# Attention 0 of a two-layer adaLN block: each group of values issued in two halves, copies of V and of the output turns moved by a slot or two

## The reference, cut to what matters

```python
h = _layernorm(x) * (1 + ca) + sa
q = (h @ Wq + bq).reshape(B, S, H, Dh)
latent = h @ Wl + bl
k = (latent @ Wk + bk).reshape(B, S, H, Dh)
v = (latent @ Wv + bv).reshape(B, S, H, Dh)
scores = einsum('bihd,bjhd->bhij', q, k) * SCALE
attn = softmax(scores)
out = einsum('bhij,bjhd->bihd', attn, v).reshape(B, S, D) @ Wo + bo
x = x + ga * out
```

## Time and profile before

| what | us |
|---|---|
| median of 3 runs | 915.63 |
| lowest and highest run | 914.82, 916.39 |
| the profiled execution | 914.76 |
| its span, first to last instruction | 912.9 |
| busy in the span: PE, DVE, ACT, POOL | 751.2, 623.3, 574.9, 326.9 |

### The profile page before, as it was taken

How to read it: one execution, slowest core, us unless ns; L and a number is a source line. 1 busy time by engine, 2 the same in 40 slices (tenths; PEclk the granted TensorE clock), 3 DMA queues, 4 the chain that set the end, 5 groups by cost and what they waited for, 6 DMA issues and landing times. The chain is left out here.

```text
span 912.9 us, 17945 instructions
## 1 busy us (share of the span) xinstructions
PE 751.2 (82%) x6002; PEld 546.6 (60%) x6002; DVE 623.3 (68%) x1509; ACT 574.9 (63%) x1285; POOL 326.9 (36%) x412
## 2 busy tenths in 40 slices
PE   3466888888588874679999999589999985999996
PEld 3222444444244333579999998467777764887874
DVE  3075787787577826677777775357676855888885
ACT  0214777777477774548888887377767743555553
POOL 3541324224221000140000000367778552776674
PEclk9999999999899997779999999789999986999999
DMA  5354353443865020000000000000000070355430
GB/s 135 34 59 49 54 55 44 53 52 48 157 121 61 8 34 17 1 1 1 1 1 1 1 1 2 1 1 2 2 1 1 3 188 4 104 146 154 114 107 23
DMA packets 78221, 42.05 MB, mean 46 GB/s; under 512 B 8649, under 2 KB 76082, under 8 KB 78002
## 3 DMA queue, kind: packets, MB, share of 16 engines
q1 hardware_dynamic: 78130, 40.89, 24.4%
HBM read 25.66 MB, written 2.24 MB: 31 GB/s over the span
## 5 line engine op out<-in xcount | busy, mean ns | idle before, releaser
L563 DVE TENSOR_REDUCE att_negmax<-att_p_max 128x2 f32<-128x512 f32 x256 | 164.6, 685 | 85.0 <-PE att_p_max L443 84.1
L647 ACT ACTIVATE att_probs<-att_p_sT 128x1024 f32<-128x1024 f32 x128 | 129.3, 1021 | 56.0 <-PE att_p_sT L449 55.1
L443 PE MATMUL att_p_max<-att0p_QK 48*128 48x256 bf16 x512 | 91.9, 290 | 36.8 <-DVE att_negmax L563 12.0
L2141 POOL TENSOR_TENSOR moe_z_lo<-moe_z,moe_z_hi 128x512 fp32r<-128x512 f32 x64 | 96.7, 1523 | 54.9 <-ACT moe_z_hi L2094 54.1
L449 PE MATMUL att_p_sT<-att0p_QK 51*128 51x256 bf16 x512 | 85.6, 279 | 1.2 <-DMA att0p_QK<-att_maxT 1.2
L933 PE MATMUL ffn0s_p_h<-ffn0s_u_hi,ffn_h_hi 128*128 128x256 f32 x256 | 71.5, 313 | 18.1 <-DVE ffn0s_u_lo L1200 12.8
L443 PEld LDWEIGHTS att_p_max<-att0p_QK 48*128 48x128 bf16 x512 | 33.6, 97 | 86.8 <-DVE att_negmax L563 47.4
L472 PE MATMUL att_p_o<-att_probs,att0p_V 128*32 128x256 f32 x1024 | 70.2, 393 | 9.5 <-ACT att_probs L647 8.4
L1200 DVE TENSOR_TENSOR ffn0s_g_lo<-top_raw,ffn0s_g_hi 128x512 fp32r<-128x512 f32 x64 | 50.4, 804 | 38.4 <-ACT ffn0s_g_hi L1145 37.1
L2132 DVE TENSOR_TENSOR moe_z<-moe_act_u,top_raw 128x512 f32<-128x512 f32 x64 | 73.7, 1151 | 2.2
L729 POOL TENSOR_TENSOR att_rstd<-att_var_eps,top_minus_half 128x2 f32<-128x2 f32 x16 | 11.5, 719 | 172.3 <-DVE att_var_eps L556 172.3
(11 more groups left out here) (273 smaller groups left out, 2047.6 us busy)
## 6 DMA issues: line engine op xcount, KB each, us to landing
top_raw<-combine SPq DMA_DIRECT2D x32, 512.0 KB, 6.5
att0p_QK<-att_parts SPq DMA_DIRECT2D x192, 64.0 KB
top_X<-in_L_attn_x SPq DMA_DIRECT2D x4, 512.0 KB, 6.9
top_raw<-in_L_ffn_h_w SPq DMA_DIRECT2D x2, 1024.0 KB
out_x<-top_X SPq DMA_DIRECT2D x8, 256.0 KB, 2.3
top_wo_all<-gates SPq DMA_DIRECT2D x1, 1024.0 KB, 5.9
prep_wmod<-in_L_wmod SPq DMA_DIRECT2D x2, 384.0 KB, 3.6
top_raw<-in_L_ffn_w_w SPq DMA_DIRECT2D x3, 256.0 KB
```

The costliest lines, as they stand in the source:

```text
L443: mm = pe.matmul(p_max[u % 2][:, i, :], QK[r][rows, g, 0, i * P:(i + 1) * P], QK[r][rows, g, 1, :], start=True, stop=True)
L563: dve.tensor_reduce(negmax[:, :, w, g], p_max[u % 2][:], AX.X, ALU.max, negate=True).then_inc(maxed, 1)
L647: act.activation(probs[g % 2][:, t % 2], p_sT[t % 2][:], ACT.Exp).then_inc(exped, 1)
L2141: pool.tensor_tensor(z_lo[e % RING][:], z[e % RING][:], z_hi[e % RING][:].bitcast(F32), ALU.subtract).then_inc(z_lo_ready, 1)
```

## The change

Three tables get new entries, and `pe_pv` gets an argument j, the key tile, so that one call issues four of the eight matmuls of a group. The waits of the group stand ahead of its first half, the signal behind its second.

- PE, values: group 0 of batch s from slot 11 to slots 11 and 12; group 1 from slot 15 to slot 15 and slot 0 of the next step; group 2 from slot 3 to slots 3 and 4; group 3 from slot 7 to slots 7 and 8. The score tiles of the later slot stand between the halves.
- PE, turns: turn of O1 from slot 9 to 10, turn back from 11 to 12, out from 12 to 13, turn of y from 14 to 15.
- DVE: second normalisation of O from ahead of tile 10 to ahead of tile 11.
- ACT: copy of V from slot 7 to 9, which is from ahead of exp1 to behind it; OTn from 11 to 12, y from 12 to 13. OT0 from slot 11 to 12, behind exp3; OT1 from slot 15 to slot 0 of the next step, behind exp5; OT2 from slot 3 to 4, behind exp7; OT3 from slot 6 to 8, behind exp1.

```diff
-PES = {"ln": 0, "max_turn": 2, "qk": 3, "O0": 5, "v": 8, "O1": 9, "back": 11, "out": 12, "turn_y": 14,
-       "pv_s": (11, 15), "pv_t": (3, 7)}
-DVE = {"negmax": 0, "stats": 2, "O0": 6, "O1": 10, "add": 15}
-ACTS = {"hT": 0, "maxT": 1, "qk": 3, "v": 7, "OTn": 11, "y": 12, "OT_s": (11, 15), "OT_t": (3, 6)}
+PES = {"ln": 0, "max_turn": 2, "qk": 3, "O0": 5, "v": 8, "O1": 10, "back": 12, "out": 13, "turn_y": 15,
+       "pv_s": {11: (0, 0), 12: (0, 1), 15: (1, 0)}, "pv_t": {0: (1, 1), 3: (2, 0), 4: (2, 1), 7: (3, 0), 8: (3, 1)}}
+DVE = {"negmax": 0, "stats": 2, "O0": 6, "O1": 11, "add": 15}
+ACTS = {"hT": 0, "maxT": 1, "qk": 3, "v": 9, "OTn": 12, "y": 13, "OT_s": {12: 0}, "OT_t": {0: 1, 4: 2, 8: 3}}
...
-        def pe_pv(pe, b, r, g):
-            if g == 0:
-                pe.wait_ge(v_ready, b + 1)
-            pe.wait_ge(exped, PAIRS * b + 2 * g + 2)
-            at_least(pe, OT_ready, 4 * b + g)
-            for j in range(NT):
-                for h in range(4):
-                    mm = pe.matmul(p_o[32 * h:32 * h + 32, 0:S], V[r][:, j, 4 * g + h, :],
-                                   probs[g % 2][:, h // 2, h % 2, j, :], start=(j == 0), stop=(j == NT - 1))
-            mm.then_inc(pv_made, 1)
+        def pe_pv(pe, b, r, g, j):
+
+            if j == 0:
+                if g == 0:
+                    pe.wait_ge(v_ready, b + 1)
+                pe.wait_ge(exped, PAIRS * b + 2 * g + 2)
+                at_least(pe, OT_ready, 4 * b + g)
+            for h in range(4):
+                mm = pe.matmul(p_o[32 * h:32 * h + 32, 0:S], V[r][:, j, 4 * g + h, :],
+                               probs[g % 2][:, h // 2, h % 2, j, :], start=(j == 0), stop=(j == NT - 1))
+            if j == NT - 1:
+                mm.then_inc(pv_made, 1)
```

More of the change, by code:

```diff
@@ L519, in pe_step @@
                 if slot in PES["pv_s"] and batch_valid(s):
-                    pe_pv(pe, s, rs, PES["pv_s"].index(slot))
+                    pe_pv(pe, s, rs, *PES["pv_s"][slot])
                 if slot in PES["pv_t"] and batch_valid(t):
-                    pe_pv(pe, t, rt, 2 + PES["pv_t"].index(slot))
+                    pe_pv(pe, t, rt, *PES["pv_t"][slot])
                 if slot == PES["O0"] and batch_valid(t):
@@ L685, in act_step @@
                 if slot in ACTS["OT_s"] and batch_valid(s):
-                    act_OT(act, s, ACTS["OT_s"].index(slot))
+                    act_OT(act, s, ACTS["OT_s"][slot])
                 if slot in ACTS["OT_t"] and batch_valid(t):
-                    act_OT(act, t, 2 + ACTS["OT_t"].index(slot))
+                    act_OT(act, t, ACTS["OT_t"][slot])
         def sp_max(sp, b, r):
```

## The result

The changed kernel takes 973.63 us (median of 4 runs, 965.35 to 979.44) against 915.51 before: a ratio of 1.0628, 95% interval 1.0549 to 1.0706. It is slower, as forecast, but by 58 us instead of 22, and outside the range. The profiled execution took 973.25 us with a span of 971.4. Its mean granted TensorE clock is 0.913 where it was 0.951, and the slowest run has the lowest of the four (0.905 at 979.44 us), the fastest the highest (0.918 at 965.35).

What follows compares the result with a forecast made beforehand. The step was taken as bound by a chain between PE and ACT. Segments summed to +1.87 us a step, 22.4 over twelve; with -1.9, +1.0 and +1.3 elsewhere, 22.8 more, so 937.5 us, range 925 to 945.

Steps and rivals of the forecast that it cites:

- 1. ln to q and k: PE, start of ln to start of q and k: values ahead of tiles1 and OT1 ahead of maxT add 0.87 us.
- 4. tiles9 to turn of O1: PE, tiles9 to turn of O1: the turn waits for V's copy, now behind exp1 and OT3 on ACT; +1.76 us.
- 5. turn of O1 to tiles12: PE, turn of O1 to tiles12: tiles10, a whole group and turn back leave, DVE wait is gone; -1.46 us.
- 6. tiles12 to tiles15: PE, tiles12 to tiles15: now holds group 0's second part, turn back to out, out and tiles14; +0.25 us.
- 7. tiles15 to ln: PE, tiles15 to ln: y's turn directly ahead of ln, so DVE's addition is no longer covered; +0.35 us.
- half group: Four of a group's eight value matmuls on PE: taken at 0.50 us, bounds 0.43 to 0.59; -0.2 to +0.3 a step.
- The clock: Rival: new 1.5 us PE waits drop TensorE to half rate for the work after them; 32 us more, 970; chance 0.03.
- steps 16 and 17: Steps without q, k and V, where turn of O1 still waits for exp1 and OT3: +0.5 us each, -0.5 to +1.0.
- steps 18 and 19: Together with step 3, lengthened by the same wait of the turn of O1: +1.3 us in all, 0 to 2.5.
- The wait in step 13: Long wait ended by a transfer burst issued in step 12; swallows about one step's loss, -1.9 us, 0 to -4.
- V and OT1 slip into gaps: Faster rival: these ACT copies cost the chain nothing and DVE's waits shrink; step 0.4 to 0.8 us shorter, 906; chance 0.07.
- either delay recovered: Rival: only one of two ACT delays bites, the one at q and k recovered; step +1.0 us, 929; chance 0.08.

Runs made afterwards that it cites:

- V ahead: The changed kernel with the copy of V and OT3 put back ahead of exp1 on ACT (slots 7 and 6): 939.33 us, ratio 1.0233.
- copies alone: The kernel before, groups unsplit, with only the copy of V, OT3 and the turn of O1 moved as in the change: 942.57 us, ratio 1.0268.
- group 1 whole: The changed kernel with group 1 unsplit in slot 15 again and OT1 in slot 15: 961.64 us, ratio 1.0476.
- filler run: The changed kernel with idle f32 matmuls in two PE waits, three ahead of q and k, four ahead of the turn of O1: 953.73 us, ratio 1.0390.
- halves alone: The kernel before with groups 0, 2 and 3 split, group 1 unsplit, all turns and copies where they were: 922.14 us, ratio 1.0043.

## Why the prediction was wrong in size

**The chain, segment by segment.** At full clock, in us, from the timeline above (the earlier trace rows for before):

| segment | before | forecast | measured |
|---|---|---|---|
| 1. ln to q and k | 2.45 | 3.32 | 3.39 |
| 2. q and k to group 3 | 5.15 | 5.15 | 5.24 |
| 3. group 3 to tiles9 | 1.87 | 1.97 | 2.11 |
| 4. tiles9 to turn of O1 | 0.31 | 2.07 | 2.09 |
| 5. turn of O1 to tiles12 | 2.93 | 1.47 | 1.48 |
| 6. tiles12 to tiles15 | 2.35 | 2.60 | 2.66 |
| 7. tiles15 to ln | 1.61 | 1.96 | 2.11 |
| step | 16.67 | 18.54 | 19.08 |

The mechanism was right in every segment, and the experiments that undo or isolate a segment (V ahead, copies alone, group 1 whole) gave the step within 0.2 us. The other signs held as well: DVE's share of a step fell from 0.78 to 0.71, and its longest idle stretch (1.06 us) is ahead of the second normalisation, if barely (1.04 ahead of tile 8). The mis-sized term is the half group: "A half group I take at 0.50, half of 1.00". It holds PE 0.57 us (157.21 to 157.78), so the two halves take 1.14 where the whole group takes 1.00. 0.57 lay inside the bounds given (0.43 to 0.59). Six halves lie on the chain (one each in segments 1, 5, 6 and 7, two in segment 3), which is up to 0.4 of the 0.54 us missing in a step. The 0.54 make 6.5 us in twelve steps, more than the upper bound of 0.3 a step that the prediction gave to this term.

**The clock, some 19 us in steps 4 to 15 and more behind.** This is the step that failed. The prediction saw the mechanism, priced it at 32 us more and gave it 0.03, because "PE stays busy over two thirds of my longer step, which speaks against it". A busy share over a whole step is no evidence on what happens around one wait: the steps at full clock show PE busy for 14.76 of 19.08 us, and their neighbours with the same work fell to 0.92 and 0.76. What the rival cost in steps 4 to 15 is 16.1 us in the eleven plain steps and, by the filler run, some 2.8 in step 13 (27.76 against 24.92). That the kernel takes about the 970 that the rival gave is luck: its 32 us were too much, and the missing ones came from the chain, from steps 16 and 17 and from the order in steps 18 and 19.

The rows that the prediction used showed 1.00 with waits of up to 0.62 and 0.80 around one of 7.72; new waits of 1.2 and 1.5 lay in that gap, and a gap in the evidence should have had a fair chance, not 0.03. The trace of before held one more row, from steps 18 and 19, which the prediction did not look at:

```profile
321.40:345.00 23.60, 16.18 (x174) 7.33 (x170) 3.98 (x19) 15.27 (x24) 0.00 (x0) 1.00 0.25 48
```

```profile
326.17 0.48 PE L449 MATMUL att_p_sT<-att0p_QK 51*128 51x256 bf16 x4 [1.23 <-DMA att0p_QK<-att_maxT]
```

That wait of 1.23 us left the clock at 1.00. Read alone it speaks for the forecast. With the traces of the changed kernel beside it, it says that a wait of this length lowers the clock in some places and not in others.

The Trainium skill (TensorE: Matmul & The Clock Gate, "What's actually happening") says that the gate goes by how busy PE has been of late; the filler run agrees with it, with 1.00 in every plain step once the waits were filled. The range ended at 945 although the rival stood at 970.

**Steps 18 and 19: 10.3 us against 1.3 with step 3.** There is no batch m and no f in them, so PE has less to put between its waits. PE's timeline of the changed kernel:

```profile
377.87 0.63 PE L484 MATMUL att_p_m<-top_ident,att_OT 128*128 128x128 f32 x4 [1.47 <-ACT att_OT L654]
...
388.99 1.08 PE L473 MATMUL att_p_o<-att_probs,att0p_V 128*32 128x256 f32 x8 [1.05 <-ACT att_OT L654]
```

Moving OT1, OT2 and OT3 behind exponentials makes every group wait for the copy of the one before, and the clock is down as well (a half group at 1.08). With fillers ahead of the turn of O1 these steps still took 30.7 us, 6.5 more than before, at a granted clock of 0.86. So at least 3.7 of the 10.3 (34.4 less 30.7) is clock and at most 6.5 is order; the runs do not part the rest. The prediction did not walk through these steps; it guessed them.

**The wait in step 13.** "About one step's loss is swallowed, -1.9": measured -0.3, within the bounds of 0 and -4, but by two errors that offset each other. With the waits filled, in the filler run, the step is 5.8 us over a plain one where it was 9.0, so about 3.1 were swallowed, and the low clock of the changed kernel gave some 2.8 back. Steps 16 and 17 gave 2.6 instead of 1.0, above the upper bound of 2.0, at a clock of 1.00.

**The rivals.** That V and OT1 slip into gaps did not happen: ACT was idle 1.80 us ahead of exp1, and the copy stood behind it. Nor was either delay recovered. That the halves gain something by feeding DVE is shown false for this chain by the halves alone, +0.27 us a step.

## What to carry to other kernels

Where several engines each have slack, take a step apart into segments on one engine's timeline and read the order of the other engines' lists: a short copy that somebody waits for belongs ahead of a long operation whose input isn't there yet (maxT and the copies of q and k moved ahead: -1.4%; V and OT3 moved behind: most of +6%). And after working out new waits of TensorE, price the clock as a case of its own: waits of 1.2 to 1.4 us, or three of 0.5 to 0.8 close together, were enough here in some steps and not in others, and filling such a wait with matmuls that nobody needs tells in one run whether it is the clock.

## What the runs showed of the hardware

- The granted clock fell to half after waits far shorter than the 7.72 us that the trace of before had: 1.22 us (some 0.8 us into it), 1.41 us, and in the kernel with the copies alone 0.62, 0.56 and 0.74 us within five microseconds. It then stayed at 0.50 for nearly 7 us (106.2 to 113 us in the changed kernel, with PE busy from 106.6 on) or for 17 (120 to 137, across the next waits for the addition and for maxT).
- The same waits one step later often did nothing, and the trace of before has one of 1.23 us at 1.00. The time of the changed kernel also spreads more: 965 to 979 us in 4 runs, where the kernel before took 913.1 to 921.1 in over 30.
- Fillers of 1.16 and 0.94 us that left 0.32 and 0.35 us of each wait were enough to keep it at 1.00, and made a kernel with more matmuls 20 us faster.
- Four f32 matmuls of 32x256 on four column groups hold PE 0.57 us, eight of them 1.00.
